# Graph attention on one core: VectorE reads the weights of gathered rows from a PSUM bank instead of from SBUF

## What is computed

```python
# layer 0: e = leaky_relu(a_src[src] + a_dst[dst]), 8 heads of 16 features
m = segment_max(e, dst);  p = exp(e - m[dst]);  denom = segment_sum(p, dst)
out = segment_sum((p / denom[dst])[:, :, None] * h[src], dst) + bias
# layer 1: score = (q[dst] . k[src]) / 4 + edge_attr @ We + be
m = segment_max(score, dst);  exp_s = exp(score - m[dst]);  ssum = segment_sum(exp_s, dst)
out = segment_sum((exp_s / (ssum[dst] + 1e-8))[..., None] * v[src], dst) @ Wo + bo
# then layer norm of (out + residual), times gamma, plus beta
```

## Time and profile before

| | us |
|---|---|
| median of 3 runs | 1489.17 |
| lowest and highest | 1487.93, 1490.18 |
| the profiled execution | 1486.06 |
| its span | 1484.3 |
| busy: PE, DVE, ACT, POOL | 980.2, 929.5, 636.9, 1190.4 |

### The profile page before, as it was taken

One profiled execution on the slowest core, in us unless ns is written; L12 is line 12 of the kernel. 1 busy time (PEld: TensorE's weight loads), 2 busy tenths in 40 slices (PEclk: granted clock), 3 DMA queues, 4 the chain that ended last, 5 costly groups with the idle time before them and its releaser, 6 DMA issues.

```text
span 1484.3 us, 21963 instructions
## 1 busy us (share of the span) xinstructions
PE 980.2 (66%) x4985; PEld 817.4 (55%) x4985; DVE 929.5 (63%) x3002; ACT 636.9 (43%) x1699; POOL 1190.4 (80%) x1806
## 2 busy tenths in 40 slices
PE   5547557777667776676575766676676856566674
PEld 4335446656555565564355655666565746455564
DVE  6446556665665666567834666666666666666578
ACT  5624343453434434341367343444445344444404
POOL 5888888888888888884048888888888888888820
PEclk9655555555555555555686778786867688787765
DMA  6332222222223222222133333333333233333311
GB/s 141 72 69 47 71 49 53 63 71 48 70 48 70 48 69 48 63 48 75 57 112 93 89 88 90 86 89 89 90 89 88 87 89 89 89 89 87 89 29 44
DMA packets 54209, 110.41 MB, mean 74 GB/s; under 512 B 16876, under 2 KB 30848, under 8 KB 53956
## 3 DMA queue, kind: packets, MB, share of 16 engines
q0 software_dynamic: 36288, 91.12, 23.5%
q1 hardware_dynamic: 16483, 17.39, 4.3%
q10 hardware_dynamic: 1313, 0.50, 0.1%
HBM read 100.60 MB, written 8.81 MB: 74 GB/s over the span
## 4 chain that ended last, share of the span: by engine, by line
POOL 39%; issue 6%; DVE 5%; PE 3%; ACT 1%; DMA 0%; DVEq 0%; POOLq 0%; SPq 0%; ACTq 0%
POOL G L511 29%; POOL pad_i L497 10%; PE bank L851 2%; DVE halves L1074 1%; DVE acc L1432 1%; DVE PV L1405 0%; DVE mv L1081 0%; DVE G L1572 0%; DVE hn L1580 0%; DVE xs L1526 0%; DVE hn L1525 0%; DVE hn L1524 0%; PE bank L899 0%; DVE G L1569 0%; DVE hn L1523 0%
## 5 line engine op out<-in xcount | busy, mean ns | idle before, releaser
L511 POOL DMA_INDIRECT G<-table,idx_all x880 | 870.6, 989 | 143.2 <-issue 124.0
L851 PE MATMUL bank<-PV,S 128*125 128x144 f32 x1760 | 446.0, 413 | 135.8 <-DVE PV L1405 74.8
L851 PEld LDWEIGHTS bank<-PV,S 128*125 128x125 f32 x1760 | 369.5, 284 | 164.1 <-issue 121.4
L1432 DVE TENSOR_TENSOR acc<-acc,bank 125x144 f32 x880 | 259.5, 295 | 235.1 <-PE bank L851 154.8
L497 POOL MEMSET pad_i<- 1x300 int32 x880 | 297.1, 338 | 18.8 <-DMA table<-h0b 9.8
L615 ACT ACTIVATE S<-iota_n,lid 128x125 f32<-128x125 f32 x880 | 275.8, 387 | 0.5 <-DVE pen L1169 0.5
L834 PE MATMUL bank<-qe,ST 125*128 x880 | 144.5, 316 | 40.1 <-DVE prod L1225 22.7
L1405 DVE TENSOR_TENSOR PV<-G,PV 128x512 f32<-128x512 f32 x220 | 150.2, 684 | 19.6 <-issue 19.4
L619 ACT ACTIVATE S<-S,ones 128x500 f32<-128x500 f32 x220 | 156.6, 712 | 7.2
L628 ACT ACTIVATE ST<-bank 125x512 f32<-125x512 f32 x110 | 62.6, 596 | 218.7 <-PE bank L899 119.1
L834 PEld LDWEIGHTS bank<-qe,ST 125*128 125x128 f32 x880 | 126.2, 221 | 50.5 <-issue 49.5
(11 more groups left out here) (220 smaller groups left out, 1257.9 us busy)
## 6 DMA issues: line engine op xcount, KB each, us to landing
G<-table,idx_all POOLq DMA_INDIRECT x880
prod<-in_edge_attr_dram SPq DMA_DIRECT2D x8, 672.0 KB
table<-G SPq DMA_DIRECT2D x12, 224.0 KB
bias_rows<-qe SPq DMA_DIRECT2D x1, 1664.0 KB, 5.8
table<-h0b SPq DMA_DIRECT2D x8, 178.5 KB
out_dram<-G SPq DMA_DIRECT2D x8, 168.0 KB
prod<-in_edge_attr_dram SPq DMA_DIRECT2D x8, 90.0 KB
xs<-in_x_dram SPq DMA_DIRECT2D x1, 504.0 KB
```

The lines of the kernel that those rows point to most:

```text
L511: pool.indirect_dma_start(G[:, u, v, 0:w], None, table, bass.IndirectOffsetOnAxis(ap=idx_all[:, g * GV + v:g * GV + v + 1], axis=0)).then_ ...
L851: last = pe.matmul(sums_bank(p)[0:BN, at:at + H * SLOT], S[:, ur, v, :], PV[:, v, :, :].rearrange("p h k -> p (h k)"), start=True, stop=True)
L1432: ve.tensor_tensor(a, a, o, ALU.add).then_inc(s.sem["acc_added"], 1)
```

## The change

`weigh` takes its second operand from sT's columns 256 to 383, where TensorE's transposes left the weights, instead of from ScalarE's copy of them in PV. The copy itself stays, as the sums read it, and so does the wait for it. Since TensorE and, in layer 0, ScalarE work on the same bank at the start of a step, the weigh also waits until the scores of group q are transposed (layer 1) or until esT is copied (layer 0). For the first quarter that would put the wait ahead of the compare and the maximum, so weigh(0) is moved behind `node_rows(1)`, `load_offsets(1)` and `loop_max()`.

```diff
+                p_edges = sT[:, 2 * P:3 * P].rearrange("p (v h) -> p v h", h=H)
...
                         wait(ve, s["pcols"], r + 1)
+                        if mid:
+                            wait(ve, s["scoreT" if n else "esT_ready"], q + 1)
                         wait(ve, s["mm_done"], sums_done(r - 1, NB - 1))
                         c0 = F if n else 0
                         rows = G[:, ur, QV * j:QV * j + QV, c0:c0 + F].rearrange("p v (h d) -> p v h d", h=H)
                         ve.tensor_tensor(PV[:, QV * j:QV * j + QV, :, 0:DH], rows,
-                                         PV[:, QV * j:QV * j + QV, :, DH:DH + 1].to_broadcast([P, QV, H, DH]), ALU.mult).then_inc(s.sem["pv_ready"], 1)
+                                         p_edges[:, QV * j:QV * j + QV, :].unsqueeze(3).to_broadcast([P, QV, H, DH]), ALU.mult).then_inc(s.sem["pv_ready"], 1)
...
                     load_offsets(0)
-                    weigh(0)
                     node_rows(1)
                     load_offsets(1)
                     loop_max()
+                    weigh(0)
                     weigh(1)
```

## The result

The changed kernel takes 1460.27 us (median of 4 runs, 1458.26 to 1464.54) against 1489.03 us (1487.93 to 1490.18, 4 runs): ratio 0.9817, 95% interval 0.9802 to 0.9831. Forecast were 1467.5 us, range 1461 to 1478, against the 1489.17 us shown then. The profiled execution took 1464.54 us (span 1462.8), where the sum of the prediction gave 1464.5. That agreement is in part luck: the profiled execution was the slowest of the four, 4.3 us above the median. Ratios are of the runs within 1.5% of the fastest of their kernel on their chip, while the medians given are of all runs, except for the kernel before on the fourth chip, where five of eleven runs lie beyond that.

What follows compares the result with a forecast made beforehand. GpSimd's stream of gathers was taken as the bound inside the layers. -24.1 + 1.0 + 1.5 = -21.6 us on the profiled 1486.06 gave 1464.5 us, 1467.5 on the median of 1489.17; range 1461 to 1478 (8 in 10).

Steps and rivals of the forecast that it cites:

- The bound and what holds a gather up: GpSimd's gathers set each layer's pace; VectorE instructions with two SBUF operands hold them up, 33.9 us in all.
- The operand: Weighs reading PSUM keep about 0.68 us and free 91 held-up gathers: -24.6 us, of which -24.1 us on the path.
- The other gathers: Gathers held by other two-operand instructions: -1 us in layer 1, +2 in layer 0 (bounds 5 and 12, taken 8.5).
- The order: Moving weigh 0 delays first sums 0.87 us a group in layer 0, 0.2 in layer 1, covered by slack.
- The tails: At layer ends nothing covers the delay: 0.8 us a layer at most, +1.5 us in all (bounds 0 and 3).
- The slack: VectorE's waits for landings, 3.5 us a group in layer 0 and 2.4 in layer 1, shrink but stay.
- A: The forecast as reasoned, gathers freed with GpSimd setting the pace: 1467.5 us, own range 1461 to 1475; chance 0.78.
- B: Layer 1's new gather pattern locks onto another two-operand instruction, costing 8 to 12 us: about 1478 us; chance 0.12.
- C: No change, 1489 us: something else about weighs holds gathers, or GpSimd waits for pv_ready instead; chance 0.05.
- D: Slower, some 1508 us: VectorE's loop becomes the bound, through weighs of 1.4 us or scores 3 us late; chance 0.05.
- the 0.90 for "faster": Whole kernel: chance 0.90 of being faster by more than 0.2% (3 us), the outcomes A and B together.

Runs made afterwards that it cites:

- plain_copy: Kernel before, but in layer 1 ScalarE copies the weights a second time, unstrided, into an SBUF tile that the weigh reads; 1489.02 us, ratio 0.9997.
- slow pace: Second memset (100 elements) ahead of each gather, added to the kernel before (1676.44 us) and to the changed kernel (1664.19 us, 0.9927 of the other).
- order_only: Changed kernel with its new order and waits, but the weigh's operand in SBUF as before; 1500.15 us, 1.0063 of the kernel before.
- old_order: Changed kernel, operand in PSUM, but weigh(0) back at its old place; 1538.77 us, 1.0326 of the kernel before.
- after_again: The changed kernel unaltered, on the second chip; 1557.83 us against 1490.57 us of the kernel before, ratio 1.0454.
- after_third: The changed kernel unaltered, on the third chip; 1546.05 us, 1.0393 of the kernel before.
- layer1_only: Changed kernel, but layer 0's weighs read PV in SBUF, so only layer 1 has the PSUM operand; 1526.78 us, 1.026 of the kernel before.
- last_two: Kernel before in its old order, but weighs 2 and 3 of each group read the PSUM bank; 1519.97 us, ratio 1.0202.
- after_fast_pace: Changed kernel with the memset ahead of each gather cut from 300 to 240 elements, fourth chip; 1790.57 us, 1.1465 of the kernel before.
- before_as_run: The kernel before unaltered, traced on the third chip; 1488.13 us, ratio 1.0009.

## Why the prediction was right, and what it missed

**The bound and what holds a gather up**: right. The second operand in SBUF was the cause (plain_copy), the weighs' share of the lateness went to nothing, and where GpSimd sets the pace a microsecond of gather is about one of span (-16.5 and -16.3 at the slow pace; -25.5 and, of the streams, -24.5 in the first comparison).

**The operand, -24.1 us**: right. 677 ns a weigh, within the lower bound; the repeated element costs nothing extra from PSUM.

**The other gathers, +1.0 us**: wrong in sign. They hold 5.8 us where they held 8.7 (layer 0 3.9 instead of the 8.5 taken, under the lower bound of 5; layer 1 1.9 instead of 1). In return the median gather takes 955 ns instead of 952, 2.6 us over 880. Together with the operand the forecast was -23.1 and the streams gave -24.5.

**The order**: half wrong. The wait for the transposed scores costs next to nothing, as forecast (1.1 us in one place). But "the instructions behind weigh 1 start when they did" fails in layer 1: the scan L1302 starts 3.76 us after the score sum instead of 3.22, 0.54 us later. The cause is the two offset loads. The second used to stand between the weighs and was worked off partly while weigh 0 ran; now both stand back to back with VectorE idle, 1.20 us instead of 0.32 + 0.26. The runs bear this out: from the score sum to the first edge scan the median is 3.75 to 3.76 us in every kernel with the new order, order_only with its SBUF operand included, and 3.23 to 3.29 in every kernel with the old one, old_order with its PSUM operand included. I counted only that 0.27 us of loads moved ahead of weigh 0. This costs nothing inside a layer while there is slack.

**The tails, +1.5 us**: too small, 2.7 us between the layers and at the end, 3.0 with the start (the bound was 3). The 0.54 us a step is the likely reason; that it is all of it isn't shown. The stream's -1.4 us beyond its forecast and these 1.5 us cancel: that is why the sum of 1464.5 us was met so closely, and it is luck.

**The medians**: their gain is 28.8 us, the traces' 21.5 of span, the forecast's 21.6. Nothing shows where the other 7 us lie, as the three faster executions of the changed kernel have no trace.

**The slack**: forecast to shrink to 2 to 2.7 us a group in layer 0 and 1.5 to 1.8 in layer 1; it was 4.9 and 2.7. The traces were not of like kind: that of before had 270 us of late signals, that of after none. I had worked out the slack from a trace in which they were already late, and had not noticed them: its additions wait 30.6 us for "remote".

**The rivals**: A was right in the comparison forecast, at 7 us more gain than its time. B and C did not occur there; the wait of GpSimd for pv_ready, which C names, is what the slower chips show (47 to 51 us). D was given 0.05 and its outcome, VectorE's loop as the bound and a loss, is what after_again, old_order and after_third showed on two chips: 1.033 to 1.045, 1539 to 1558 us, more than D's 1508. So the changed kernel was slower on two of the three chips on which it ran as it is; the 0.90 for "faster" was worked out from one trace on one chip, and that the forecast comparison ran on a chip of the good kind is luck as well. But its mechanism is another one. It asked for weighs of 1.4 us or transposed scores 3 us late; the weighs take 677 to 679 ns there too. TensorE's signals come late there, by up to some 8 us, and VectorE's additions wait 103 to 135 us for them: that is what lengthens the loop, as far as the waits show it. The step of the argument that fails on those chips is "the saved time comes off the path as long as VectorE still waits for landings": with a faster stream of gathers the consumers don't keep their duration.

**What stays open**: why TensorE's signals come late, why on some chips or in some executions and not in others, and why a faster GpSimd makes it so much worse than the time it gives. Shown is that at a pace slow enough no signal is late, with either operand, and that at the faster pace they are late with either operand. That the operand adds something of its own at the standard pace isn't excluded: the slow pair had no lateness that it could have increased, and layer1_only and last_two, where the loss follows the operand, have faster gathers wherever they have the operand. A kernel with the PSUM operand and a spacer longer by just the 30 ns a gather that it gains would tell the two apart; it wasn't run. On the fourth chip there is no trace at the standard pace. No version was found that beats both kernels on every chip; a memset between 300 elements and the slow pace's two wasn't tried, and neither was the pair of weighs ahead of both offset loads.

## What to carry to other kernels

A gather by GpSimd that starts under a VectorE instruction with two SBUF operands is held, here until some 0.56 us into a 128x512 fp32 product of 0.68 us; one operand moved to PSUM frees it (the instruction itself took 677 ns instead of 684), and where GpSimd is the bound that is the gain. But in a pipeline whose bound is a steady producer, the bound also spaces out the consumers' work: before a faster producer is counted as a gain, read from the trace how late TensorE's signals are already (waits named remote, behind matmuls long ended), and measure on more than one chip. How far the consumers are behind is seen at a layer's end: count what is left to do once the producer's last piece has landed. Slack read from one trace is slack on one chip.

## What the runs showed of the hardware

- TensorE's signals can come microseconds behind the recorded ends of its matmuls: none of some 500 inside the layers in each slow-pace trace and in the first of after, some 190 signals with about 270 us in the first trace of before, some 250 with about 850 us in after_fast_pace, the longest 11.6 us. They are late more often behind matmuls recorded at 2.4 GHz than behind those at 1.2 GHz.
- The kernel before took 1489 to 1491 us in three comparisons and 1558 us in the fourth, on another chip; the changed one 0.982, 1.039 and 1.045 of the kernel before.
- On the fourth chip 45 us less work for GpSimd made the kernel some 120 us slower, and some 0.2 us more a gather some 118 us (1677.72 and 1676.44 us against 1558.1): the standard pace lies between two slopes.
- Two loads of offsets into VectorE's registers that stand back to back, with nothing running, leave it idle for 1.20 us; with a weigh between them the idle time is 0.58 us in all.
- The Trainium skill, "SBUF — State Buffer", section "Who interferes with whom", infers that descriptor generation isn't stalled by a tensor_tensor with both inputs in SBUF. The runs contradict it: of layer 1's gathers that start at a weigh 57 are late in before_as_run, by 14.6 us, and 41, by 11.0 us, with an unstrided SBUF operand in plain_copy, against at most 3, by 0.1 us, in each trace with a PSUM operand there.
